# Decoder kernel: expert weights laid out by partition and issued at the logits stage's begin, row stores and a norm on ScalarE, moved loads, waits and bias adds

## Chip, core and metric

The kernel runs on one core of one Trainium2 chip, in one launch. The metric is device time in microseconds (us). The engines are TensorE (PE in the rows; PEld is its weight load), VectorE (DVE), ScalarE (ACT), GpSimd (POOL) and SyncE (SP, which here only issues DMAs).

## Reference

A post-norm decoder of two layers, x of shape (2, 1024, 256), context of shape (2, 154, 192), 16 heads of 16 channels, everything float32. Cut to what matters:

```python
x = layernorm(x + alibi_attention(x))      # half the heads forward, half backward, biased
x = layernorm(x + cross_attention(x, ctx)) # scores clipped to +-10000
x = layernorm(x + moe(x))                  # softmax router, 8 experts, top 2,
                                           # (gelu(x w1) * (x v1)) w2, w1 and v1 256x704, w2 704x256
x = layernorm(x + attention(x))            # full
x = layernorm(x + cross_attention(x, ctx)) # no clip
h = x + mla(rmsnorm(x))                    # causal, keys and values from a latent of 128
x = layernorm(x + h + moe(rmsnorm(h)))     # 8 experts, top 2, silu(x w1) w2, w1 256x512, w2 512x256
```

## The kernel before

The rows of x (2048 tokens of 256 floats) live in SBUF as x_tok, 16 tiles of 128 tokens; two tiles are a pair. The program is a list of 17 stages that run one after another. A counter, stage_done, stands between them (lines 2412 to 2426): each of the five engines ends its part of a stage, drains, adds one, and waits at the next stage until all five have done so. A stage may name one engine that adds its one without draining ("undrained"), and may give SP work that comes behind its drain ("sp_behind"), beside which the other engines go on. The stages are:

- **t0, t1, t4, t5**: token stages (token_stage, line 697). They add the attention's output projection to x, normalise, transpose, and multiply with weights for queries, keys and values, which SP stores to DRAM in the layout that the next stage loads (q_halves, k_parts). A planner (path_lengths, order_by and list_order, lines 93 to 160) sets each engine's order from a table of tasks with costs. t0 also computes keys and values of the context for both cross-attentions (ContextPart), stores the values (line 1284), and loads x (line 1268).
- **at0, at1, mla**: self-attention (self_attention_stage, line 1418): score matmuls of a key block (L1515, L1539, L1542) into one of three PSUM banks, exponential on ScalarE (L1598) into one of four probability buffers, probability-value matmuls (L1557), row maxima on VectorE (L1631), which POOL splits into bfloat16 parts (L1646 to L1653) and SP moves back to be used as an extra row of the next job's scores (L1440). SelfAttention.plan (line 202) writes out the order of these events on TensorE. After the first split POOL adds the projection's bias of the next stage to x_tok (add_bias, L1393: four adds of 128x1024).
- **xa0, xa1**: cross-attention, in sixteen jobs with the same split (L1733 to L1746). xa0 clips the scores: VectorE applies it in L1884. POOL adds the bias after its second split.
- **t2, t6**: token stages whose only product are router logits. After the norm of each pair (task "keep") SP stores that pair's rows to DRAM (x_rows, L841) and then issues a part of the expert weights (between_sp, L2337 to L2355).
- **rt0, rt1**: routing: VectorE picks experts and ranks tokens; POOL's gathers from x_rows (L2088) fetch the tokens of the first experts. SP issues the last four down-projection weights of layer 0 in rt0.
- **ex0, ex1**: experts over 78 tiles of tokens, 39 in each layer; TensorE's first matmul in them is a transpose of fetched rows (L2163).
- **t3, t7**: combine stages (source "comb"): two y rows a token are loaded (y_rows, L834), VectorE adds them with gate weights (L1119), takes mean and variance (L1131, L1134), ScalarE the root (L956), VectorE the reciprocal (L1139) and the norm (L1144). t3 goes on to queries, keys and values; t7 stores the output (L846).

## Time and profile before

| | us |
|---|---|
| median of three runs | 2222.88 (2217.84 to 2225.1) |
| the profiled execution | 2224.16 |
| its span in the profile | 2222.4 |
| TensorE busy in the span | 1953.6 |
| mean granted clock of TensorE | 0.925 of 2.4 GHz |

The stages' begins in the profiled execution, in us of its span: t0 4.4, at0 87.8, t1 364.6, xa0 409.9, t2 558.3, rt0 592.4, ex0 616.8, t3 970.7, at1 1045.4, t4 1462.4, xa1 1506.6, t5 1614.1, mla 1688.1, t6 1955.5, rt1 1991.9, ex1 2013.8, t7 2187.0.

The table by stage gives each engine's busy time in a stage. Where TensorE is busy nearly throughout, only its own idle gaps can be won; where it is not, the timeline and the waits at that place name what it waits for. A group's mean is the price of one instruction. In a timeline row the first number is the start, the second the time that the instructions merged in it took; the bracket has the idle time before them, and what released the engine.

### The profile page before, as it was taken

What the parts mean: (1) busy time and instruction counts of PE and PEld (TensorE: products, weight loads), DVE (VectorE), ACT (ScalarE), POOL (GpSimd) and SP (SyncE); (2) the same over time, 40 slices, a digit from 0 to 9 for tenths busy, and PEclk for the clock granted to TensorE, in tenths of its full rate; (3) what the DMA queues carried; (4) which work ended last, traced back from release to release, by engine and by line L of the source; (5) the groups of instructions that cost most, each with busy time, mean ns of one, the idle gap of its engine ahead of it and who ended that gap; (6) DMA issues with size and microseconds to landing.
All of it is one profiled execution on the core that took longest, in us unless ns stands there. A gap on an engine that the chain in (4) does not pass through costs nothing. (4 is left out here: it accounts for less than half of the span.)

```text
span 2222.4 us, 32846 instructions
## 1 busy us (share of the span) xinstructions
PE 1953.6 (88%) x10990; PEld 1004.1 (45%) x10991; DVE 1294.2 (58%) x2318; ACT 999.2 (45%) x1921; POOL 477.6 (21%) x801
## 2 busy tenths in 40 slices
PE   8699999688669999967999999997887999977992
PEld 4344445333546666643222222253453444464662
DVE  3478784687612222246888888745576887653115
ACT  2156665377211111123466666763542666632331
POOL 2220011522123222212100000023242011033441
PEclk9689999799779999988799999997997999987996
DMA  8522312421730101136211111034225333052223
GB/s 220 137 50 46 62 32 45 101 55 21 278 115 28 33 28 33 28 117 147 34 29 30 30 30 30 2 87 101 46 73 107 59 59 59 2 166 66 63 64 128
DMA packets 111607, 157.90 MB, mean 71 GB/s; under 512 B 31543, under 2 KB 88695, under 8 KB 108535
## 3 DMA queue, kind: packets, MB, share of 16 engines
q1 hardware_dynamic: 103986, 135.75, 26.9%
q0 software_dynamic: 7488, 20.46, 3.0%
q8 instruction: 74, 1.21, 0.3%
q14 instruction: 59, 0.48, 0.1%
HBM read 110.44 MB, written 44.72 MB: 70 GB/s over the span
## 5 line engine op out<-in xcount | busy, mean ns | idle before, releaser
L1598 ACT ACTIVATE arena<-psum 128x512 f32<-128x512 f32 (+1 forms) x1120 | 574.6, 591 | 360.9 <-PE psum L1539 184.2
L1631 DVE TENSOR_REDUCE arena<-psum 128x1 f32<-128x1024 f32 (+3 forms) x352 | 399.9, 1172 | 94.0 <-PE psum L1515 64.9
L1515 PE MATMUL psum<-arena 96*128 96x512 bf16 (+7 forms) x1280 | 366.6, 369 | 31.0 <-DVE arena L1674 12.0
L1539 PE MATMUL psum<-arena 99*128 99x512 bf16 (+7 forms) x1280 | 366.0, 353 | 21.7 <-DMA arena<-arena 13.5
L1617 DVE CUSTOM_DVE_ANT_0 arena<-psum,arena 128x640 bf16<-128x640 f32 (+3 forms) x256 | 250.1, 1022 | 66.6 <-PE psum L1515 65.3
L1557 PE MATMUL psum<-arena 128*32 128x512 f32 (+3 forms) x2560 | 281.5, 538 | 1.1 <-ACT arena L1598 1.1
L2175 PE MATMUL psum<-arena 128*128 x780 | 270.5, 493 | 1.9 <-ACT arena L2229 1.2
L1515 PEld LDWEIGHTS psum<-arena 96*128 96x128 bf16 (+1 forms) x1280 | 100.8, 100 | 272.9 <-issue 82.4
L1539 PEld LDWEIGHTS psum<-arena 99*128 99x128 bf16 (+1 forms) x1280 | 124.6, 99 | 195.9 <-ACT arena L1598 76.4
L2279 DVE COPY arena<-psum 128x640 f32<-128x640 f32 (+1 forms) x78 | 59.3, 760 | 252.6 <-PE psum L2185 252.6
L2194 PE MATMUL psum<-arena 128*128 (+1 forms) x780 | 189.1, 384 | 2.1 <-DVE arena L2282 1.2
L2175 PEld LDWEIGHTS psum<-arena 128*128 128x128 f32 x780 | 143.6, 192 | 82.6 <-issue 25.0
L1646 POOL CAST arena<-arena 32x128 bf16<-32x128 f32 x48 | 13.5, 282 | 757.5 <-DVE arena L1638 757.5
L2194 PEld LDWEIGHTS psum<-arena 128*128 128x128 f32 (+1 forms) x780 | 138.3, 189 | 30.8 <-issue 16.0
L1064 PE MATMUL psum<-arena 128*128 128x512 f32 x240 | 115.2, 621 | 17.3 <-DMA arena<-in_xT 9.8
L2272 DVE TENSOR_TENSOR arena<-arena,psum 128x704 f32<-128x704 f32 x39 | 34.7, 891 | 164.0 <-PE psum L2175 164.0
L2088 POOL DMA_INDIRECT arena<-x_rows,arena x78 | 75.8, 972 | 241.8 <-PE psum L2163 206.6
L1868 DVE TENSOR_REDUCE arena<-psum 128x4 f32<-128x616 f32 x128 | 100.2, 796 | 39.8 <-PE psum L1767 39.2
L1852 ACT ACTIVATE arena<-psum 128x512 f32<-128x512 f32 x160 | 93.7, 604 | 41.8 <-PE psum L1785 40.3
L2124 POOL DMA_INDIRECT y_rows<-arena x78 | 77.0, 987 | 159.0 <-ACT arena L2246 158.7
L1557 PEld LDWEIGHTS psum<-arena 128*32 128x32 f32 x2560 | 59.8, 108 | 111.0 <-issue 65.6
L1542 PE MATMUL psum<-arena 128*128 128x128 bf16 x512 | 98.4, 221 | 0.0
(206 smaller groups left out, 2360.7 us busy)
## 6 DMA issues: line engine op xcount, KB each, us to landing
arena<-k_parts SPq DMA_DIRECT2D x144, 128.0 KB
q_halves<-arena SPq DMA_DIRECT2D x80, 192.0 KB, 3.2
arena<-q_halves SPq DMA_DIRECT2D x40, 384.0 KB, 4.8
arena<-q_halves SPq DMA_DIRECT2D x40, 256.0 KB, 5.2
k_parts<-arena SPq DMA_DIRECT2D x48, 192.0 KB, 3.2
arena<-in_L_ffn_w SPq DMA_DIRECT2D x9, 1024.0 KB, 12.8
arena<-y_rows SPq DMA_DIRECT2D x32, 256.0 KB, 4.1
arena<-in_L_ffn_w SPq DMA_DIRECT2D x8, 704.0 KB, 11.3
```

The costliest lines, as they stand in the source:

```text
L1064: last = nc.tensor.matmul(ps[:, :], m, xt[:, c, :], start=(c == 0), stop=(c == DC - 1))
L1515: last = nc.tensor.matmul(dst[:, base + lo:base + hi], q[0:rows, qh, h, qb % 4 * P:qb % 4 * P + P], k[0:rows, h, key0 + lo:key0 + hi], sta ...
L1539: last = nc.tensor.matmul(b[:, at0:at0 + width], kk[0:rows, h, kb * P:kb * P + P], q[0:rows, qh, h, c0:c1], start=True, stop=diag is None)
L1542: last = nc.tensor.matmul(b[:, at0 + diag - c0:at0 + diag - c0 + P], identb, mask_right if at.modes[g] == "bwd" else mask_left, start=Fals ...
L1557: last = nc.tensor.matmul(bank[o_bank][32 * h:32 * h + 32, c0:c1], v_st[g % 2][:, kb, h, :], probs[k % 4][:, h, c0:c1], start=first, stop=end)
L1598: nc.scalar.activation(probs[k % 4][:, heads[0]:heads[-1] + 1, c0:c1], bank[st_bank[no % 3]][:, 0:len(heads) * width].rearrange("p (h q) - ...
L1617: last = nc.vector.tensor_tensor_reduce(out=unread[:, turn % 2, n_h * width:n_h * width + width], in0=src[:, n_h * pitch:n_h * pitch + wid ...
L1631: nc.vector.tensor_reduce(dst, src, AX.X, ALU.max).then_inc(t("taken"), 1)
L1852: nc.scalar.activation(place(j, tile), src, ACT.Exp, scale=QSCALE).then_inc(t("p"), 1)
L1868: nc.vector.tensor_reduce(dst, src, AX.X, ALU.max).then_inc(t("taken"), 1)
L2175: last = nc.tensor.matmul(bank[2 * w + hf][:, 0:half], xT[:, s, c, :], wu[:, ds(e, 1), c, w, hf * half:hf * half + half].rearrange("p o f ...
L2194: last = nc.tensor.matmul(bank[7][:, 0:D], hT[0:fw[f], s, f, :], w2[f][0:fw[f], ds(e, 1), :].rearrange("p o d -> p (o d)"), start=(f == 0) ...
```

## The change

Ten edits; three places where they move instructions are shown behind the diff.

1. The expert weights are laid out so that each partition reads one run: first-layer w1 and v1 together (8 DMAs of 128x2816 elements in place of 16 of 128x2x704), w2 (rows of 2048 elements). All between_sp work stands behind the drain of SP in t2 and t6.
2. The row stores of t2 and t6 are issued by ScalarE (store_rows, task "keep").
3. In combine stages VectorE computes the reciprocal and minus mean times reciprocal (dve_shift); ScalarE applies scale and shift to the two tiles of a pair (act_norm).
4. Combine stages name POOL as the engine that isn't drained.
5. x is loaded in at0, behind its weights 2, in place of t0.
6. The wait for the context's stores (stored) goes from the end of t0 to the begin of t1; VectorE waits for the value stores before it writes its first output of at0.
7. at0 and mla use five probability buffers; at1 keeps four. The plan holds a score back until fewer than that many products are open, and gives products a later due time for pairs.
8. The bias of both cross-attentions is added after the last split, in 16 adds of 128x256. In self-attention it stays.
9. Lines 112 and 113 of the changed kernel raise the rank of one task; SP's order is not moved by it.
10. TensorE waits for the up weights of layer 0 by the new count of DMAs.

```diff
@@ -243,7 +246,7 @@
             if n_st < len(st):
                 k, n = st[n_st]
                 j = self.steps[k][0]
-                if j in landed:
+                if j in landed and len(pvs) > k - self.ahead:
                     ready.append((max(landed[j], exps[n_st - 3] if n_st > 2 else 0.0), at[k] + n * took[k] / HG, "ST"))
             if n_mx < len(mx):
                 _, j, n = mx[n_mx]
...
@@ -260,7 +263,7 @@
                 j = self.steps[n_pv][0]
                 if len(exps) >= done and (j == 0 or len(copied) >= j):
                     ready.append((max(exps[done - 1], copied[j - 1] if j else 0.0), 
-                                  at[n_pv + self.pair - 1] + 1.6 * took[n_pv + self.pair - 1], "PV"))
+                                  at[n_pv + self.pair - 1] + 1.6 * self.pair * took[n_pv + self.pair - 1], "PV"))
             open_now = [(k, r, w) for r, k, w in ready if r <= now + 0.05]
             if open_now:
                 _, _, what = min(open_now)
...
@@ -752,7 +755,8 @@
                             task("POOL", "spread", p, 1.05, 0.2, ("moments", p))
                         else:
                             task("ACT", "root", p, 0.35, 0.15, ("moments", p))
-                        task("DVE", "norm", p, 0.85 if source == "proj" else 1.1, 0.15, ("spread", p), ("root", p))
+                            task("DVE", "shift", p, 0.45, 0.15, ("root", p), ("norm", p - 4))
+                        task("DVE" if source == "proj" else "ACT", "norm", p, 0.85, 0.15, ("spread", p), ("shift", p))
                     if rms is not None:
                         if norm:
                             task("DVE", "again", p, 1.25, 0.15, ("norm", p), ("rms", p - 4))
@@ -764,7 +768,7 @@
                         task("PE", "trx", p, 0.55, 0.2, (normed, p), ("xts", p - 2))
                         task("ACT", "xts", p, 0.65, 0.15, ("trx", p), ("unit", half_end(p // 2 - 2) - 1))
                     if between_sp:
-                        task("SP", "keep", p, 2.5, 2.0, (normed, p))
+                        task("ACT", "keep", p, 0.6, 2.0, (normed, p))
                     if final:
                         task("SP", "final", p, 0.5, 2.0, ("norm", p))
                 for u, (kind, o, f, part) in enumerate(units):
...
                         load_rows(sp, n)
                         if n == 3 and wn is not None and next_weights:
                             load_weights(sp, wn + 1)
-                    elif kind == "keep":
-                        store_rows(sp, n)
-                        if n + 1 < n_pairs:
-                            between_sp(sp, n)
                     elif kind == "final":
                         store_out(sp, n)
                     elif kind == "store":
@@ -882,10 +882,9 @@
             def sp_stored(sp):
...
                     sp.wait_ge(out_sem(place), stored(nqk))
-                if context:
-                    context.stored(sp)
                 if between_sp:
-                    between_sp(sp, n_pairs - 1)
+                    for p in range(n_pairs):
+                        between_sp(sp, p)
 
             def pool_third(pool, u):
                 n = qk_no[u]
...
@@ -956,6 +955,13 @@
                 nc.scalar.activation(rstd[:, 0, ring(p)], mv[:, 0, ring(p), 1], ACT.Sqrt,
                                      bias=eps_col[:, 0:1]).then_inc(t("root"), 1)
 
+            def act_norm(act, p):
+                act.wait_ge(t("shift"), p + 1)
+                for u in (2 * p, 2 * p + 1):
+                    nc.scalar.activation(x_tok[:, u, :], r_tok[:, u % TPB, :], ACT.Identity,
+                                         bias=rstd[:, 1, u % TPB:u % TPB + 1], scale=rstd[:, 0, u % TPB:u % TPB + 1])\
+                        .then_inc(t("xs"), 1)
+
             def act_xts(act, p):
                 act.wait_ge(t("trx_ps"), p + 1)
                 if p >= 4:
...
@@ -1133,13 +1143,16 @@
                     hold(dve, t(f"st{n}"), 2 * p + i + 1, t("held_dve"))
                     nc.vector.bn_aggr(mv[:, n, 2 * (p % 4) + i, :], bst[:, n, 2 * (p % 4) + i, :]).then_inc(t(done), 1)
 
+            def dve_shift(dve, p):
+                dve.wait_ge(t("root"), p + 1)
+                nc.vector.reciprocal(rstd[:, 0, ring(p)], rstd[:, 0, ring(p)]).then_inc(t("inverse"), 1)
+                dve.wait_ge(t("inverse"), p + 1)
+                nc.vector.scalar_tensor_tensor(out=rstd[:, 1, ring(p)], in0=mv[:, 0, ring(p), 0], scalar=-1.0,
+                                               in1=rstd[:, 0, ring(p)], op0=ALU.mult, op1=ALU.mult)\
+                    .then_inc(t("shift"), 1)
+
             def dve_norm(dve, p):
-                if source == "comb":
-                    dve.wait_ge(t("root"), p + 1)
-                    nc.vector.reciprocal(rstd[:, 0, ring(p)], rstd[:, 0, ring(p)]).then_inc(t("inverse"), 1)
-                    dve.wait_ge(t("inverse"), p + 1)
-                else:
-                    dve.wait_ge(t("pool_n"), 2 * p + 2)
+                dve.wait_ge(t("pool_n"), 2 * p + 2)
                 for u in (2 * p, 2 * p + 1):
                     nc.vector.tensor_scalar(x_tok[:, u, :], r_tok[:, u % TPB, :], mv[:, 0, u % TPB, 0:1],
                                             rstd[:, 0, u % TPB:u % TPB + 1], ALU.subtract, ALU.mult)\
...
@@ -1223,6 +1238,8 @@
                         context.dve_values(dve, n)
 
             progs = {"sp": sp_prog, "dve": dve_prog, "pool": pool_prog, "act": act_prog, "sp_behind": sp_stored}
+            if source == "comb":
+                progs["undrained"] = "pool"
             if units or source == "proj":
                 progs["pe"] = pe_prog
             stages.append((name, progs))
...
@@ -1265,7 +1282,6 @@
             def load(self, sp):
                 load_context_rows(sp)
                 load_weights(sp, self.wn)
-                sp.dma_start(x_tok, a["x"].rearrange("b (t p) d -> p (b t) d", p=P)).then_inc(sem("x_loaded"), 16)
 
             def store(self, sp, n):
                 t, (l, f) = self.t, self.kunits[n]
...
-                sp.wait_ge(t("vstored"), 16 * 2)
+            def values_stored(self, eng):
+                eng.wait_ge(self.t("vstored"), 16 * 2)
+
+            def stored(self, eng):
+                self.values_stored(eng)
                 for s in range(2):
-                    sp.wait_ge(t(f"scr{s}"), 16 * 4 * 2)
+                    eng.wait_ge(self.t(f"scr{s}"), 16 * 4 * 2)
 
             def pe_keys(self, pe, n):
                 t, ct, (l, f) = self.t, self.ct, self.kunits[n]
...
@@ -1385,13 +1403,13 @@
 
         biased = [0]
 
-        def add_bias(pool, n, row):
+        def add_bias(pool, n, row, step=4):
 
             weights_ready(pool, n)
             pool.wait_ge(sem("x_loaded"), 16)
-            for p in range(0, NT, 4):
-                nc.gpsimd.tensor_tensor(x_tok[:, p:p + 4, :], x_tok[:, p:p + 4, :],
-                                        row.unsqueeze(1).to_broadcast([P, 4, D]), ALU.add)\
+            for p in range(0, NT, step):
+                nc.gpsimd.tensor_tensor(x_tok[:, p:p + step, :], x_tok[:, p:p + step, :],
+                                        row.unsqueeze(1).to_broadcast([P, step, D]), ALU.add)\
                     .then_inc(sem("bias_added"), 1)
                 biased[0] += 1
 
...
@@ -1752,8 +1774,8 @@
                         .then_inc(t("pads"), 1)
                 for j in range(len(at.jobs)):
                     pool_split(pool, j)
-                    if j == 1 and bias:
-                        add_bias(pool, *bias)
+                if bias:
+                    add_bias(pool, *bias, 1)
 
 
             def pe_max(pe, j, n):
...
@@ -2336,26 +2358,24 @@
 
         def up_weights0(sp, first, end):
             for e in range(first, end):
-                for w, src in enumerate((g("L0_ffn_w1"), g("L0_ffn_v1"))):
-                    sp.dma_start(wu0[:, e, :, w, :], src[e].rearrange("(c p) f -> p c f", p=P)).then_inc(sem("up0"), 16)
+                sp.dma_start(wu0[:, e].rearrange("p c w f -> p (c w f)"), g("L0_ffn_up")[:, e, :]).then_inc(sem("up0"), 16)
             if end == NX:
                 down_weights0(sp, (4, 5))
 
         def down_weights0(sp, chunks):
             for n in chunks:
                 r = min(P, F0 - n * P)
-                sp.dma_start(w2_0[n][0:r, :, :], g("L0_ffn_w2")[:, n * P:n * P + r, :].rearrange("e p d -> p e d"))\
+                sp.dma_start(w2_0[n][0:r].rearrange("p e d -> p (e d)"), g("L0_ffn_down")[n * P:n * P + r, :])\
                     .then_inc(sem("down0"), 16)
 
         def weights1(sp, e):
-            sp.dma_start(wu1[:, e, :, 0, :], g("L1_ffn_w1")[e].rearrange("(c p) f -> p c f", p=P))\
-                .then_inc(sem("up1"), 16)
+            sp.dma_start(wu1[:, e].rearrange("p c w f -> p (c w f)"), g("L1_ffn_up")[:, e, :]).then_inc(sem("up1"), 16)
             for n in range(4 if e == NX - 1 else 0):
-                sp.dma_start(w2_1[n], g("L1_ffn_w2")[:, n * P:n * P + P, :].rearrange("e p d -> p e d"))\
+                sp.dma_start(w2_1[n].rearrange("p e d -> p (e d)"), g("L1_ffn_down")[n * P:n * P + P, :])\
                     .then_inc(sem("down1"), 16)
 
         def weights0_wait(pe):
-            pe.wait_ge(sem("up0"), 16 * 2 * NX)
+            pe.wait_ge(sem("up0"), 16 * NX)
             pe.wait_ge(sem("down0"), 16 * 6)
 
...
-        self_attention_stage(at0, (2, W["t1"]["brow"]), lambda sp: load_weights(sp, 2))
+                     ("v", w["wv"], w["bv"])], w, following=at0, context=context_part)
+        def rows_and_weights(sp):
+            load_weights(sp, 2)
+            sp.dma_start(x_tok, a["x"].rearrange("b (t p) d -> p (b t) d", p=P)).then_inc(sem("x_loaded"), 16)
+
+        self_attention_stage(at0, (2, W["t1"]["brow"]), rows_and_weights, context_part.values_stored)
         w = W["t1"]
+
+        def first_context(sp):
+            context_part.stored(sp)
+            load_context(sp, 0)
+
         token_stage("t1", 2, "proj", True, None, [("qk", w["wq"], w["bq"], q_halves)], w,
-                    early_sp=lambda sp: load_context(sp, 0), following=xa0)
+                    early_sp=first_context, following=xa0)
         cross_attention_stage(xa0, (3, W["t2"]["brow"]))
         w = W["t2"]
         token_stage("t2", 3, "proj", True, None, [("logits", w["router"], logits)], w,
```

SP, from the last issues in t2 into rt0, before (x_rows is the store of rows, in_L_ffn_w and in_L_ffn_v are expert weights):

```order
L2340 DMA arena<-in_L_ffn_v 128x2x704
L841 DMA x_rows<-arena 128x2x256
L2340 DMA arena<-in_L_ffn_w 128x2x704
L2340 DMA arena<-in_L_ffn_v 128x2x704
L2347 DMA arena<-in_L_ffn_w 128x8x256
L2347 DMA arena<-in_L_ffn_w 64x8x256
L2347 DMA arena<-in_L_ffn_w 128x8x256 x4
L615 DMA arena<-in_L_attn_W_qkv 128x2x256 x3
```

The same place in the changed kernel, from the last moves of xa0 on:

```order
L1736 DMA arena<-arena 1x16x128 x12
L2361 DMA arena<-in_L_ffn_up 128x2816 x8
L2368 DMA arena<-in_L_ffn_down 128x2048
L2368 DMA arena<-in_L_ffn_down 64x2048
L2368 DMA arena<-in_L_ffn_down 128x2048 x4
L618 DMA arena<-in_L_attn_W_qkv 128x2x256 x3
L618 DMA arena<-in_L_attn_b_qkv 128x256
```

No row store stands on SP any more; all up weights and two down weights follow on each other, with the four others behind the next stage's begin.

POOL in xa0, before, at the end of the second split:

```order
L1744 CAST arena<-arena 32x128
L1746 TENSOR_TENSOR arena<-arena 32x128
L1393 TENSOR_TENSOR arena<-arena 128x1024 x4
L1733 TENSOR_SCALAR arena<-arena 32x128
L1739 CAST arena<-arena 32x128
L1741 TENSOR_TENSOR arena<-arena 32x128
```

POOL in xa0, after, from the end of the last split into t2 (ISA rows are semaphore clears between stages):

```order
L1763 TENSOR_TENSOR arena<-arena 32x128
L1766 CAST arena<-arena 32x128
L1768 TENSOR_TENSOR arena<-arena 32x128
L1411 TENSOR_TENSOR arena<-arena 128x256 x16
L2449 ISA x26
L898 TENSOR_SCALAR arena<-arena 128x2
L901 TENSOR_TENSOR arena<-arena 128x2
```

The adds have left the stretch between split two and three and stand behind the last one, in sixteen pieces.

VectorE in t7, before, from its first combining adds:

```order
L1119 SCALAR_TENSOR_TENSOR arena<-arena 128x256 x8
L1131 BN_STATS arena<-arena 128x6 x2
L1134 BN_AGGR arena<-arena 128x2 x2
L1131 BN_STATS arena<-arena 128x6 x2
L1134 BN_AGGR arena<-arena 128x2 x2
L1139 RECIPROCAL arena<-arena 128x2
L1144 TENSOR_SCALAR arena<-arena 128x256 x2
L1139 RECIPROCAL arena<-arena 128x2
L1144 TENSOR_SCALAR arena<-arena 128x256 x2
```

VectorE in t7, after:

```order
L1129 SCALAR_TENSOR_TENSOR arena<-arena 128x256 x16
L1141 BN_STATS arena<-arena 128x6 x2
L1144 BN_AGGR arena<-arena 128x2 x2
L1141 BN_STATS arena<-arena 128x6 x2
L1144 BN_AGGR arena<-arena 128x2 x2
L1148 RECIPROCAL arena<-arena 128x2
L1150 SCALAR_TENSOR_TENSOR arena<-arena 128x2
L1141 BN_STATS arena<-arena 128x6 x2
L1144 BN_AGGR arena<-arena 128x2 x2
L1129 SCALAR_TENSOR_TENSOR arena<-arena 128x256 x4
```

The norms of 128x256 are gone from VectorE, a 128x2 row stands behind each reciprocal, and the first adds are taken four pairs at once.

## Rows read from the trace of the kernel before

**Rows 1.** page, part 1: busy us (share), instructions
```profile
PE 1953.6 (88%) x10990; PEld 1004.1 (45%) x10991; DVE 1294.2 (58%) x2318; ACT 999.2 (45%) x1921; POOL 477.6 (21%) x801
```

**Rows 2.** table by stage (us, busy (x), clock, DMA share, GB/s): t2, rt0
```profile
558.30:592.40 34.10, 32.26 (x192) 29.29 (x192) 18.94 (x60) 13.36 (x24) 7.57 (x16) 0.86 0.70 259
592.40:616.80 24.40, 3.16 (x34) 2.23 (x34) 20.14 (x64) 0.42 (x2) 3.65 (x10) 0.50 1.07 348
```

**Rows 3.** waits, 592.4 to 640 (us in total, times, longest)
```profile
ACT arena L2229 <- PE psum L2163: 32.8, 2, 30.4
```

**Rows 4.** timeline (start, us, engine, line, operation, [idle before <-releaser]), rt0 to ex0
```profile
614.17 0.17 DVE L2045 TENSOR_TENSOR arena<-arena 128x16 f32<-128x16 f32 x1
...
626.88 0.66 PE L2163 MATMUL psum<-arena 128*128 128x128 f32 x2 [14.68 <-DMA arena<-in_L_ffn_w]
```

**Rows 5.** timeline, the same place in layer 1, rt1 to ex1
```profile
2013.52 0.18 DVE L2045 TENSOR_TENSOR arena<-arena 128x16 f32<-128x16 f32 x1
...
2017.12 0.69 PE L2163 MATMUL psum<-arena 128*128 128x128 f32 x2 [5.45 <-DMA arena<-x_rows,arena]
```

**Rows 6.** timeline of SP, t2 and rt0
```profile
568.43 0.38 SPq L841 DMA_DIRECT2D x_rows<-arena  x1
...
583.08 1.64 SPq L841 DMA_DIRECT2D x_rows<-arena  x1
...
595.66 21.00 SPq L2347 DMA_DIRECT2D arena<-in_L_ffn_w  x6
```

**Rows 7.** DMA, 592 to 616.9, in 40 equal slices
```profile
GB/s 414 412 416 402 412 393 378 429 389 414 409 403 389 383 424 417 410 403 398 380 363 356 346 345 334 178 179 204 189 181 220 296 332 327 339 321 337 345 349 341
```

**Rows 8.** timeline, end of t3 and start of at1
```profile
1036.80 2.14 POOL L894 TENSOR_TENSOR arena<-arena 128x512 bf16<-128x512 f32 x2 [1.53 <-ACT arena L984]
...
1037.92 2.55 SPq L827 DMA_DIRECT2D k_parts<-arena  x4
...
1045.48 0.11 DVE L1674 MEMSET arena<- 128x64 f32 x1 [5.38 <-POOLq L2426]
```

**Rows 9.** instruction groups (busy us, mean ns | idle before), stage t7
```profile
L1144 DVE TENSOR_SCALAR arena<-arena 128x256 f32<-128x256 f32 x16 | 5.9, 410 | 0.3
```

**Rows 10.** timelines of POOL, VectorE and TensorE, start of xa0
```profile
424.24 7.85 POOL L1393 TENSOR_TENSOR arena<-arena 128x1024 f32<-128x1024 f32 x4
...
425.63 7.01 DVE L1884 SCALAR_TENSOR_TENSOR arena<-arena 128x512 f32<-128x512 f32 x1
...
433.41 0.69 PE L1767 MATMUL psum<-arena 96*128 96x154 bf16 x4 [6.05 <-DVE arena L1868]
```

**Rows 11.** instruction groups of VectorE, 540.2 to 548.8, end of xa0
```profile
L1884 DVE SCALAR_TENSOR_TENSOR arena<-arena 128x512 f32<-128x512 f32 x5 | 3.5, 691 | 4.2 <-ACT arena L1852 4.2
```

**Rows 12.** timelines of POOL and TensorE, xa1
```profile
1520.80 7.87 POOL L1393 TENSOR_TENSOR arena<-arena 128x1024 f32<-128x1024 f32 x4
...
1528.62 0.28 POOL L1739 CAST arena<-arena 32x128 bf16<-32x128 f32 x1
...
1533.21 0.39 PE L1785 MATMUL psum<-arena 99*128 99x512 bf16 x1 [2.37 <-DMA arena<-arena]
...
1602.52 0.40 POOL L1746 TENSOR_TENSOR arena<-arena 32x128 bf16<-32x128 f32 x1
```

**Rows 13.** waits, stage t0
```profile
ACT arena L975 <- DMA q_halves<-arena: 19.8, 3, 13.2
```

**Rows 14.** table by stretch, as rows 2, end of t0
```profile
60.80:81.30 20.50, 19.68 (x58) 9.81 (x58) 8.56 (x33) 4.15 (x9) 5.49 (x6) 0.50 0.44 112
```

**Rows 15.** timelines of TensorE and POOL, start of at0
```profile
111.38 0.58 PE L1539 MATMUL psum<-arena 105*128 105x512 bf16 x1 [9.04 <-DMA arena<-arena]
...
112.57 7.88 POOL L1393 TENSOR_TENSOR arena<-arena 128x1024 f32<-128x1024 f32 x4 [14.13 <-DMA arena<-in_L_xattn_bq]
...
125.85 0.28 POOL L1646 CAST arena<-arena 32x128 bf16<-32x128 f32 x1 [5.41 <-DVE arena L1638]
```

**Rows 16.** table by stretch, as rows 2, middle of at0
```profile
112.00:345.00 233.00, 226.94 (x1796) 105.00 (x1794) 181.95 (x339) 142.44 (x279) 30.81 (x68) 0.97 0.28 45
```

40 lines of the change are left out of this document (29 added, 11 removed).

## Prediction

> **What bounds the kernel now.** I read the page first, then a table of busy time by stage, and from there only the places where TensorE stands still. TensorE is busy 88% of the span [rows 1] and the change leaves its arithmetic alone, so what can be won is idle time at joints between stages, in stages without matmuls (routing, last combine), and in stretches at 1.2 GHz that a stall brought on. The table of stages names one joint at once: routing 0 lasts 24.4 us, TensorE works 3.16 of them, and the DMA engines are full (share 1.07), as they are through most of the logits stage (0.70 over a stage whose first third has no transfer) [rows 2]. The waits behind it say what TensorE waits for: 14.7 us for expert weights [rows 3]. Everything else is smaller than 10 us and is read at its own place below.
>
> The sum is made against the profiled execution, 2224.16 us (span 2222.4); the median of the three runs, 2222.88, is 1.3 lower, and I take that off at the end.
>
> **Expert weights.** VectorE ends routing 0 at 614.17 + 0.17 = 614.34, and the first expert matmul starts at 626.88, released by the weights [rows 4]. In routing 1 the weights are there in time, and the first matmul starts 2017.12 - 2013.52 = 3.60 us after the start of the same VectorE instruction, released by the fetched rows [rows 5]. With weights in time experts 0 would start at 614.17 + 3.60 = 617.8: **-9.1**. Are they in time? Now the first weight DMA follows the first row store at 568.4, pairs of weights alternate with stores, and the last six are issued until 616.7 [rows 6]. After the change eight DMAs of 1.44 MB and two down-projection ones are issued from the stage's begin at 558.4, the other four from 592.4. Bytes: 11.5 MB up, 5.8 MB down, 2.1 MB of rows, 19.4 MB in all. The rates while the engines are full are 380 to 429 GB/s, then 178 to 220 in a dip and about 340 at the end, where the 1024-byte packets of the down weights run [rows 7]. At 400 the last byte lands at 558.4 + 48.5 = 607, at 340 at 615.5, both before 617.8; it takes under 327 GB/s to lose anything. Long rows per partition should not be slower than short ones. So the full 9.1; what is late next is the row fetch, and nothing closer than 2 us behind it.
>
> **Row stores on ScalarE** (logits stages). Eight issues of a DMA go into ScalarE's stream in t2, eight in t6. No row of before has a DMA issue on ScalarE; the nearest are SP's issues of the same store, 0.38 us with empty queues and 1.64 under backlog [rows 6]. After the change all of t2's stand under backlog. ScalarE is busy 13.36 of 34.1 us in t2, TensorE 32.26 [rows 2]: TensorE sets the stage, and ScalarE's two thirds of idle time cover 8 x 0.38 = 3 us whole, and 8 x 1.64 = 13 us in part, because the stores stand between the activations that TensorE's next transposes wait for, and wait for VectorE's norm themselves. I take **+0.5** for t2, 0 for t6 (nearer to the empty price, as the store has its own queue), bounds -1 and +9 together.
>
> What a page says to that: the Trainium skill, "DMA: Bandwidth & Descriptors", section "Issuing engines are not separate DMA queues", has DMAs of all issuing engines run on the same 16 engines and interleave, so that issuing on another one saves only the sequencer's time. That speaks against any gain in transfer from moving the stores, and by it a store would wait among 13 MB of weights; rows 7's rates make that some tens of us, which the gather at 614 can stand. It leaves the sum as it is.
>
> **The end of combine stage t3.** Its last POOL work ends at 1036.80 + 2.14 = 1038.9, SP's last store is issued by 1037.92 + 2.55 = 1040.5, yet the next stage starts at 1045.48 with VectorE released by POOL's queue at the line of the drain [rows 8]. POOL is now not drained before it reports. SP is last then, with some 0.4 us to the next instruction: 1040.9 against 1045.4, **-4.5**. Bounds -5 and -2 (if SP's or ScalarE's own drain is late too).
>
> **Last combine stage t7.** VectorE sets it. Sixteen normalisations of 0.410 us, 5.9 us busy, leave it [rows 9]; eight tiny shifts come, some 0.2 us each as its other 128x2 ones: 5.9 - 1.6 = 4.3 less work. Of that the last pair gives back 0.3 (a handoff to ScalarE before the last store) and I leave 0.7 for waits on the square root: **-3.3**, bounds -4.5 and +1. In t3, where the same sixteen leave VectorE but TensorE and four other engines share the stage, 0, bounds -2 and +1.
>
> **Late bias in cross-attention.** Before, POOL's four adds run from 424.24 for 7.85 us. VectorE's clip of line 1884, two inputs in SBUF, starts at 425.63 and takes 7.01 us; its usual time is 0.69 [rows 10, 11]. TensorE then stands for 6.05 us [rows 10]. Without the adds there: -6.2. The new place is after the last split, at 540.2, for sixteen adds of a quarter the size: 7.85 us of work plus sixteen starts, some 8.5. In that time five clips stand [rows 11], two more follow, and the chain clip, matmul, exp is what the stage's end (558.3) hangs on. The row shows VectorE shut out across the boundaries of back-to-back adds, so I expect the same again: a clip held to about 548.8, 5.6 us late, of which the 4.2 us of idle ahead of those clips can take back 1 to 2. **+3.7**, net **-2.5**, bounds -8 and +2. Cross-attention 1 has no clips. There the adds (1520.80, 7.87 us) only hold back POOL's next split to 1528.62, and TensorE's wait for the split's result is 2.37 us [rows 12]: -2.5. Its new adds run from 1602.9 to 1611.4 and the stage ends at 1614.1: hidden, with 2.7 us to spare. **-2.5**, bounds -4 and +1.
>
> The Trainium skill, "SBUF — State Buffer", section "Who interferes with whom", says that the second of a VectorE instruction with two SBUF inputs and a POOL one reading SBUF blocks until the first finishes. The row disagrees: one add takes 1.96 us, the clip was held over more than three. By the page a clip after the change would wait one small add, 0.5 us, and the end would cost about +1 in place of +3.7. That is part of rival B.
>
> **x load and context waits.** The 2 MB of x no longer stand ahead of t0's first stores, for which ScalarE waits 19.8 us in three waits [rows 13]; those come out with work beside them, and TensorE's later gap is one of VectorE's: **-1.5**, bounds -3 and 0. At at0's start SP no longer waits for the context's value stores before it loads group 1, some 3.9 us earlier; TensorE's gap of 9.04 before 111.38 waits for data from such a load [rows 15]: -3.9. But x now comes behind the attention's weights, which landed by 112.5 (ahead of 112.57 [rows 15]) and would at 108.6; its 2 MB at 340 GB/s take 6 us and more beside other loads, so about 116, and the adds, now 112.57 to 120.45, go to about 124; the next split is at 125.85 [rows 15] and would be due at 122: about +2. **-2**, bounds -5 and +1.
>
> **Plan of at0 and mla.** Five probability buffers, and probability-value matmuls placed some four places later. In the stretch after the start TensorE is busy 226.94 of 233.0 us [rows 16]; at most 6 us are idle there, and some of it are joints no order mends. I take **-2** for each of the two stages, bounds -5 and +4 each (a worse order has no ceiling but the idle time that it makes). At1's order is the same in both kernels.
>
> **Sum:** -9.1 + 0.5 - 4.5 - 3.3 - 2.5 - 2.5 - 1.5 - 2 - 2 x 2 = **-28.9**. 2224.16 - 28.9 = 2195.3, and less 1.3: **2194**.
>
> **Rivals.**
> B, more than the sum: POOL's small adds let VectorE in (+1 in place of +3.7), and in t0 or at at0's start the shorter stall leaves the clock up. The stretch 60.8 to 81.3 runs at 0.50 (1.2 GHz) and holds 19.68 us of matmuls, which at 2.4 GHz are some 10 [rows 14]. 2194 - 2.7 - 9 = 2182. For it: that stretch follows a 6 us wait. Against: the wait comes from VectorE, not from a store. Chance 0.18.
> C, ScalarE pays the backlog price: 16 issues x (1.64 - 0.38) = 20 us, half of it in front of transposes, +10: 2204. Chance 0.13.
> C', the new plan costs what it was to give, +4 in place of -2 in both stages: 2194 + 12 = 2206. Chance 0.12.
> E, the weights do not come in time, as the long rows gain nothing and rows, weights and ScalarE's queue hinder each other: the 9.1 stay, 2203. Chance 0.04.
> D, **slower**: ScalarE's store can't be issued until the weight backlog has drained. In t2 12.8 MB stand ahead at 0.4 MB/us, 32 us from 558.4; the first store is due near 568, so ScalarE, and TensorE behind it, stand 22 us, and later stores some 5; in t6 8 MB are 20 us, due 10 after the stage's begin, 10 and 4. 2194 + 41 = 2235. It decides once these stalls pass 29 us (no gain left), and is slower by the measure below from 36. Against it: SP's store under full backlog took 1.64, not tens [rows 6]. Chance 0.03.
>
> **Numbers.** Forecast 0.48 (2194), the rest as above, 0.02 for what I don't see. The range holds B's time and C' with its bounds: 2179 to 2212. A difference of 0.3% (6.7 us) is what a measurement of this kernel can tell from none; all cases but D, and the ends of C and C' together, are below 2216: faster 0.93, same 0.04, slower 0.03.
>
> **What would show it.** Routing 0 to experts 0: first matmul of experts within 4 us of routing's last VectorE instruction, released by fetched rows. T3 to at1: no 5 us wait on POOL's queue. Cross-attention 0: no clip of 7 us near 425, and clips near 543 either 0.7 or several us long (decides B's first half). T0: the clock after 60. T2: length 34 or above 40 (C, D). At0 and mla: TensorE's idle time in the middle, 6 us now. Wrong I would be above all if t2 grew by more than 5, or if a stage I hold unchanged (at1, t4, t5) moved.

## The result, and the profile after

| | before | changed |
|---|---|---|
| median, same session, us | 2221.72 (4 runs) | 2196.57 (4 runs, 2184.7 to 2198.73) |
| ratio, 95% interval | | 0.9883 [0.9858, 0.9907] |
| span of the profiled execution | 2222.4 | 2197.0 |

The forecast was 2194 (2179 to 2212), the time 2196.57. The forecast fall was 28.9 us; measured against the kernel before in the same session it was 25.2 us, and 19.8 us when the changed kernel was run again (e5). The stages say less good things of the working. The table has each stage's length from the profiled executions: before has two (its own and that of e11 below), the changed kernel has those of all the kernels below in which the stage's own instructions, in their own place and order, are the changed kernel's. A stage's length is from the moment the five engines may start it to the next such moment, for t7 to the end of the span. The mean of t0 leaves out the 68.9; with it, it is 76.5.

| stage | before | changed, number of executions, mean | difference | forecast |
|---|---|---|---|---|
| t0 | 83.4, 81.0 | 75.7 to 79.1, eight, 77.4; once 68.9 | -4.8 | -1.5 |
| at0 | 276.7, 276.8 | 272.3 to 274.6, eight, 273.6 | -3.1 | -4 |
| xa0 | 148.5, 146.8 | 144.8 to 149.5, eight, 147.0 | -0.7 | -2.5 |
| t2 | 34.0, 33.9 | 35.9 to 37.4, seven, 36.6 | +2.6 | +0.5 |
| rt0 + ex0 | 378.3, 378.5 | 368.2 to 369.5, seven, 369.1 | -9.3 | -9.1 |
| t3 | 74.7, 76.8 | 73.3 to 76.3, seven, 75.1 | -0.7 | -4.5 |
| at1 | 417.0, 415.7 | 414.5 to 416.7, twelve, 415.3 | -1.1 | 0 |
| xa1 | 107.5, 106.6 | 103.0 to 105.8, eleven, 104.6 | -2.4 | -2.5 |
| mla | 267.3, 267.2 | 266.1 to 270.3, eleven, 267.5 | +0.2 | -2 |
| t6 | 36.4, 36.4 | 33.8 to 37.5, eight, 36.8 | +0.4 | 0 |
| t7 | 35.4, 36.0 | 32.8 to 34.1, twelve, 33.4 | -2.3 | -3.3 |

The stages not listed (t1, t4, t5, rt1, ex1) have means within 0.5 us of the kernel before. The differences of the table add up to -21.2 us, against -28.9 in the forecast.

The largest term stands as it was worked out. Of the changed kernel's timeline at the end of routing 0 (columns as in rows 4):

```profile
607.43 0.17 DVE L2067 TENSOR_TENSOR arena<-arena 128x16 f32<-128x16 f32 x1
...
611.54 0.69 PE L2185 MATMUL psum<-arena 128*128 128x128 f32 x2 [6.07 <-DMA arena<-x_rows,arena]
```

The first expert matmul starts 4.11 us behind the start of routing's last VectorE instruction, released by fetched rows; in [rows 4] that was 12.71 us, released by a weight. The table by stage, t2 and rt0, answers to [rows 2]:

```profile
548.80:585.60 36.80, 35.04 (x192) 31.77 (x192) 18.88 (x60) 13.19 (x24) 7.44 (x16) 0.80 0.98 386
585.60:607.70 22.10, 3.15 (x34) 2.22 (x34) 20.07 (x65) 0.42 (x2) 1.78 (x9) 0.50 0.60 238
```

The weights now move in t2 (share 0.98 for 0.70, 386 GB/s), and routing has 0.60 where it had 1.07. T2 itself is longer, at a lower clock (0.80 for 0.86) with TensorE still busy through it: 14.9 us of it are at 1.2 GHz, for 9.4 before.

The end of t3, answering to [rows 8]: no wait for POOL's queue is left, SP is last, and the joint from VectorE's last instruction to its next takes 1.0 us for 5.4.

```profile
1026.71 0.76 DVE L1201 TENSOR_TENSOR arena<-psum,arena 128x256 f32<-128x256 f32 x2 [0.97 <-PE psum L1088]
1028.47 0.11 DVE L1696 MEMSET arena<- 128x64 f32 x1 [1.00 <-SPq L2456]
```

Cross-attention 0, the new place of the bias adds (timelines of POOL, VectorE and TensorE), answering to [rows 10]:

```profile
524.43 9.54 POOL L1411 TENSOR_TENSOR arena<-arena 128x256 f32<-128x256 f32 x16
...
527.48 7.04 DVE L1906 SCALAR_TENSOR_TENSOR arena<-arena 128x512 f32<-128x512 f32 x1 [3.28 <-ACT arena L1874]
...
536.50 1.94 PE L1828 MATMUL psum<-arena 128*32 128x512 f32 x8 [5.90 <-DVE arena L1906]
```

The stall of [rows 10] has moved, nearly to the tenth: a clip of 7.04 us for 7.01, a gap of TensorE of 5.90 for 6.05. Some ten boundaries between adds went by without letting VectorE in, and the clip ended 0.55 us behind the last add, as the clip in [rows 10] did.

Stage t0, waits and TensorE's timeline, answering to [rows 13]; and t7's groups, answering to [rows 9]:

```profile
ACT arena L981 <- DMA q_halves<-arena: 10.1, 1, 10.1
```

```profile
57.66 1.47 PE L1329 MATMUL psum<-arena 128*128 128x256 f32 x4 [1.98 <-DVE arena L1391]
```

```profile
L961 ACT ACTIVATE arena<-arena 128x256 f32<-128x256 f32 x16 | 8.5, 590 | 3.0 <-DVE arena L1150 3.0
...
L1150 DVE SCALAR_TENSOR_TENSOR arena<-arena 128x2 f32<-128x2 f32 x8 | 1.3, 163 | 0.3
```

The start of at0 (timelines of TensorE and POOL), answering to [rows 15]:

```profile
105.14 0.58 PE L1559 MATMUL psum<-arena 105*128 105x512 bf16 x1 [6.88 <-DMA arena<-arena]
...
112.04 7.88 POOL L1411 TENSOR_TENSOR arena<-arena 128x1024 f32<-128x1024 f32 x4 [17.97 <-DMA arena<-in_x]
119.86 0.28 POOL L1666 CAST arena<-arena 32x128 bf16<-32x128 f32 x1
```

### The profile page after: what moved, and what is told of

Read it like the earlier page. It is cut to its first block and busy times, and to the rows that moved or that the text cites. A ratio compares the mean times of both kernels' runs of the same rounds, so it can differ in the third digit from the quotient of the medians.

```text
span 2197.0 us, 32881 instructions
## 1 busy us (share of the span) xinstructions
PE 1950.5 (89%) x10990; PEld 1009.5 (46%) x10991; DVE 1282.9 (58%) x2302; ACT 1015.5 (46%) x1953; POOL 482.0 (22%) x825
## 5 line engine op out<-in xcount | busy, mean ns | idle before, releaser
L1559 PE MATMUL psum<-arena 99*128 99x512 bf16 (+7 forms) x1280 | 365.9, 354 | 19.4 <-DMA arena<-arena 10.5
L2197 PE MATMUL psum<-arena 128*128 x780 | 270.3, 493 | 1.7 <-ACT arena L2251 1.2
L1874 ACT ACTIVATE arena<-psum 128x512 f32<-128x512 f32 x160 | 93.6, 604 | 38.7 <-PE psum L1807 37.4
```

The costliest lines, as they stand in the source:

```text
L1559: last = nc.tensor.matmul(b[:, at0:at0 + width], kk[0:rows, h, kb * P:kb * P + P], q[0:rows, qh, h, c0:c1], start=True, stop=diag is None)
L1874: nc.scalar.activation(place(j, tile), src, ACT.Exp, scale=QSCALE).then_inc(t("p"), 1)
L2197: last = nc.tensor.matmul(bank[2 * w + hf][:, 0:half], xT[:, s, c, :], wu[:, ds(e, 1), c, w, hf * half:hf * half + half].rearrange("p o f ...
```

## The experiments

Each kernel is the changed kernel with the edit shown, unless it says otherwise. Ratios are to the kernel before in the same session.

**e1: POOL drained again in combine stages.**

```diff
-            if source == "comb":
-                progs["undrained"] = "pool"
```

> The changed kernel with POOL drained at the end of the combine stages again. In the changed kernel t3 lasts 73.3 us and at1 414.6, against 74.7 and 417.0 before. Theory (the drain is worth its wait and the clock that the wait costs): t3 grows by 4.5 us to about 77.8, VectorE again waits about 5.4 us on POOL's queue at the start of at1, and at1's start at 1.2 GHz ends some 2 to 3 us later after its begin, so at1 grows by about 2.4; time +7 (2203). Rival (at1's 2.4 us has another cause, its first loads or the state in which SP comes out of t3): t3 +4.5, at1 unchanged, time +4.5. Second rival (the drain is hidden, as other engines end later in the re-planned t3): t3 +1 to +2.

Median 2206.64, ratio 0.9944 [0.9921, 0.9967]. T3 78.94 us, at1 414.97. The wait is back (timeline of VectorE at at1's start):

```profile
1028.29 0.11 DVE L1694 MEMSET arena<- 128x64 f32 x1 [5.53 <-POOLq L2454]
```

Against the seven t3 of the changed kernel (mean 75.1) the drain costs 3.8 us, and 2.7 against the longest of them. At1 is as without it: the 2.4 us that at1 seemed to gain are not the drain's. In the stages this is the first rival. The median rose by 10 us, more than either gave; that rest is in no stage of the profile (span 2200.3 for 2197.0 and 2199.3), whose execution was the fastest of this kernel's seven, and stays open.

**e2: norm of t3 on VectorE.** The plan's tasks and dve_norm as before where the stage is not the final one.

```diff
-                            task("DVE", "shift", p, 0.45, 0.15, ("root", p), ("norm", p - 4))
-                        task("DVE" if source == "proj" else "ACT", "norm", p, 0.85, 0.15, ("spread", p), ("shift", p))
+                            if final:
+                                task("DVE", "shift", p, 0.45, 0.15, ("root", p), ("norm", p - 4))
+                        if source == "comb" and not (final):
+                            task("DVE", "norm", p, 1.1, 0.15, ("root", p))
+                        else:
+                            task("DVE" if source == "proj" else "ACT", "norm", p, 0.85, 0.15, ("spread", p), ("shift", p))
```

> The changed kernel with the norm of t3 on VectorE again (reciprocal and subtract-multiply, planned as before); t7 keeps it on ScalarE. Up to its last store t3 took 70.2 us before (1040.9 - 970.7) and 73.3 in the changed kernel. Theory (putting the norm on ScalarE costs t3 its new 3 us, as ScalarE's queue then delays the evictions that TensorE waits for): t3 falls to 70 to 71, time -3 (2193.5). Rival (the 3 us come from the start of t3, that is from the order of the first combining adds or the loads, whoever does the norm): t3 stays at 73 +-0.7. t7 32.6 +-0.3 in both.

Median 2194.04, ratio 0.9889 [0.9852, 0.9927]. T3 69.76 us; e9, e10 and e12 below, which share the edit, have 69.5, 69.7 and 68.5 (e12 has another edit in t3). So the norm on ScalarE costs t3 5 to 6 us of its 75.1, more than expected, and t7, which keeps it, stays at 33.4. Part of that is the clock: five of the changed kernel's seven t3 (75.4 to 76.3) have a second stretch of 3.4 us at 1.2 GHz near 66 us, which no t3 of these four has. Against the two without it (73.3 and 73.7) the norm costs 3.5 to 4.2 us, e12 left out. The median does not show the gain: 0.9889 lies between the changed kernel's 0.9883 and 0.9907, and only the span (2190.4 for 2197.0 and 2199.3) does. The first 20 us of t3, of this kernel and of the changed one (columns as in rows 2), show that TensorE gets less done from the start:

```profile
950.10:970.10 20.00, 8.35 (x18) 4.28 (x19) 12.81 (x38) 3.44 (x8) 0.00 (x0) 0.57 0.79 243
```

```profile
955.10:975.10 20.00, 6.11 (x13) 3.28 (x14) 12.90 (x42) 5.26 (x13) 0.00 (x0) 0.53 0.78 243
```

The groups of ScalarE over t3 have the cause as far as it shows: sixteen activations of 128x256 that take VectorE 410 ns each [rows 9] take ScalarE 591, in a queue that also holds TensorE's evictions.

```profile
L961 ACT ACTIVATE arena<-arena 128x256 f32<-128x256 f32 x16 | 8.7, 591 | 1.3 <-DVE arena L1150 1.3
```

TensorE's first matmul of t3 comes 11.5 us after the begin in the changed kernel and 10.9 here, and behind it TensorE idles 9.4 us and 6.6: together 3.4 of the 3.5 us between the two profiles. Its largest gap in t3 (3.36 us, here 1.57) stands behind VectorE, VectorE behind an eviction of ScalarE, and that behind a store of q_halves (6.79 us, here 4.31).

**e3: a wait before each late bias add.**

```diff
             for p in range(0, NT, step):
+                if step < 4 and p:
+                    pool.wait_ge(sem("bias_added"), biased[0])
```

> The changed kernel with one wait ahead of each of the sixteen bias adds in the cross-attentions: POOL waits for the add before it. In the changed kernel the adds ran 9.54 us back to back and a clip of VectorE took 7.04 us beside them. Theory (VectorE is shut out as long as POOL's adds follow each other without a pause; a wait in between lets it in): the clips take at most 1.4 us each, TensorE's gap of 5.9 us shrinks to 1 or 2, xa0 147.6 -> 143 to 144, time -4 (2192.5). Rival (it is not the queueing of adds but POOL's reading that slows VectorE, in proportion to the time shared): a clip still takes over 3 us or the sum of the clips' extra time stays near 6, xa0 unchanged. POOL's adds take longer, some 11 to 12 us in all; in xa1, with 2.7 us to spare, they may end after the others: xa1 +0 to +1.

Median 2196.94, ratio 0.9875 [0.9829, 0.9921]. Cross-attention 0 137.68 us. Timelines of POOL and VectorE at the place of the stall:

```profile
523.65 14.68 POOL L1413 TENSOR_TENSOR arena<-arena 128x256 f32<-128x256 f32 x16
...
525.88 1.08 DVE L1908 SCALAR_TENSOR_TENSOR arena<-arena 128x512 f32<-128x512 f32 x1 [3.29 <-ACT arena L1876]
...
532.79 1.02 DVE L1908 SCALAR_TENSOR_TENSOR arena<-arena 128x512 f32<-128x512 f32 x1 [1.46 <-ACT arena L1876]
```

A clip takes 0.68 to 1.13 us beside POOL's adds, against 0.69 alone and 7.04 beside adds that follow on each other; the nine clips beside them lose 2.9 us together, where the rival had 6. Being shut out is a matter of adds queued without a pause. The price is on POOL, 14.68 us for 9.54. The stage's 9.9 us are more than the stall, as its stretches at 1.2 GHz fell from 29.5 to 18.8 us in this execution; in e9, e10 and e12, with the same wait in xa0, it took 141.7, 141.4 and 143.6, against a mean of 147.0, so 3.4 to 5.6 us are the edit's. The median did not follow: t3, at1 and xa1 were 1.6 to 3.1 us longer in the profile than in the changed kernel's. For t3 and at1, not edited, that is within the scatter of the table. Xa1, which has the waits too, took 106.3 us, 0.5 over the longest without them, and ended with POOL's last add (1588.56 and 1588.63): there the waits cost something.

**e4: less weight backlog in t2.**

```diff
-                    for p in range(n_pairs):
+                    for p in range(n_pairs if name == "t6" else 5):
                         between_sp(sp, p)
...
-        routing_stage("rt0", True, "t2", "ex0", lambda sp: down_weights0(sp, (0, 1, 2, 3)))
+        routing_stage("rt0", True, "t2", "ex0", lambda sp: (up_weights0(sp, 5, NX), down_weights0(sp, (0, 1, 2, 3))))
```

> The changed kernel with the up weights of five experts issued at t2's begin and those of the last three, with the down weights, only in routing 0. t2 took 34.05 us before and 36.8 in the changed kernel, where the last two row stores held ScalarE's queue 5.7 us and the clock fell 25.3 us after t2's begin (28.1 before). 4.3 MB move by some 25 us: the last byte at about 605, first expert matmul then still released by fetched rows (611.5). Theory (backlog price): the row stores take under 1 us each, t2 falls to 34 to 35, time -2. Rival (ScalarE's place in the plan, not the backlog, costs it): t2 stays 36.5 or more. Rival (what the shorter t2 gains comes back as waiting for weights in experts 0): rt0 and ex0 together grow by the same 2.

Median 2202.01, ratio 0.9925 [0.9895, 0.9956]. ScalarE's issue of the last row store took 0.37 us, where it takes 3.70 in the changed kernel (rows under e8), and t2 stayed at 36.85 all the same: the clock had fallen 25.4 us after its begin, and TensorE's wait for ScalarE's last evictions was 0.69 us in both, as before. And the deferred weights came late (timelines of ScalarE and TensorE):

```profile
575.20 0.37 ACTq L845 DMA_DIRECT2D x_rows<-arena  x1
```

```profile
614.30 0.66 PE L2185 MATMUL psum<-arena 128*128 128x128 f32 x2 [10.43 <-DMA arena<-in_L_ffn_down]
```

That is 8.2 us after routing's end (606.07), and ex0 is 4.0 us longer. The estimate of a last byte at 605 was too early: the up weights of five experts and the rows are through by 577, and the DMA engines move nothing more until 584.

**e5: the changed kernel again,** nothing edited.

> The changed kernel once more, nothing edited, to learn how far a stage's length moves between executions of the same program. Expected by both theories: at0, t1, xa0, rt0, t7 within 1 us of 273.4, 45.0, 147.5, 22.0, 32.6; t3 either near 73.3 or near 76.2 (both lengths were seen for this code), going with the length of its stretch at 1.2 GHz (20.5 or 23.9 us); xa1 103 to 105, again with its stretch at 1.2 GHz. Theory (the kernel's total moves by several us only by which stretches the clock is low): span 2190 to 2200, and the difference to 2197.0 is found in t3, xa1, t5 and t6. Rival: the lengths are fixed, and t3's 73.3 against 76.2 in two kernels edited elsewhere is an effect of these edits; then t3 is 73.3 again.

Median 2199.65, ratio 0.9907 [0.9879, 0.9934]. Span 2199.3. T3 75.36, xa1 103.03, at0 273.74, t7 33.03, rt0 22.00; xa0 149.51, 2.0 above the first, with 38.1 us at 1.2 GHz for 29.5. So t3's 73.3 in the first profile was its short end, and a single profile tells nothing of a stage under 2 to 3 us unless the clock's stretches are the same.

**e6: x loaded in t0 again.**

```diff
                 load_weights(sp, self.wn)
+                sp.dma_start(x_tok, a["x"].rearrange("b (t p) d -> p (b t) d", p=P)).then_inc(sem("x_loaded"), 16)
...
             load_weights(sp, 2)
-            sp.dma_start(x_tok, a["x"].rearrange("b (t p) d -> p (b t) d", p=P)).then_inc(sem("x_loaded"), 16)
```

> The changed kernel with the load of x back in t0; the moved waits stay as they are. In the changed kernel t0 takes 78.4 us (83.4 before), its large gap 1.98 us in place of 6.12. Theory (x ahead of the first stores made ScalarE wait, and VectorE's late answer after it opened the gap): t0 back to 82 to 83.5, its gap 5 to 6 us. At0: bias adds begin some 5 us earlier than 29.2 us after at0's begin, at0 -1 to 0. Time +3 to +4 (2200). Rival (the gap closed because SP no longer waits at t0's end and the plan's order around it, not by x): t0 stays near 78.4.

Median 2197.66, ratio 0.9899 [0.9878, 0.992]. T0 81.04, at0 270.79. Waits of t0 and TensorE's and POOL's timelines:

```profile
ACT arena L981 <- DMA q_halves<-arena: 17.7, 3, 11.7
```

```profile
59.07 2.37 PE L1330 MATMUL psum<-arena 128*128 128x256 f32 x4 [3.58 <-DVE arena L1392]
```

```profile
107.01 7.88 POOL L1412 TENSOR_TENSOR arena<-arena 128x1024 f32<-128x1024 f32 x4 [10.50 <-DMA arena<-in_L_xattn_bq]
```

The rival is out (t0 is 1.9 above the longest with x in at0), and the theory holds in direction, not in size: x in t0 costs t0 3.7 us and saves at0 2.8, where 4 to 5 and 0 to 1 were expected, so that the move is worth under 1 us. The gap was 3.58, not 5 to 6. But the kernel before had it at 2.90 in its second execution (e11), so that the 6.12 of the forecast's rows was its long end. ScalarE's wait and TensorE's gap move together, one for one: of the thirteen executions of all kernels here with such a wait (all but e12's), twelve have a gap of the wait less 8.2 us. It is 11.07 and 2.90 in e11, 11.7 and 3.58 here, 10.1 and 1.98 in the changed kernel; the one left out has 13.2 and 6.12.

**e7: the old plan of at0 and mla.**

```diff
-        self.ahead = 4 if modes[0] == "full" else 5
+        self.ahead = 4
...
-                if j in landed and len(pvs) > k - self.ahead:
+                if j in landed:
...
-                                  at[n_pv + self.pair - 1] + 1.6 * self.pair * took[n_pv + self.pair - 1], "PV"))
+                                  at[n_pv + self.pair - 1] + 1.6 * took[n_pv + self.pair - 1], "PV"))
```

> The changed kernel with the plan of before for at0 and mla: four probability buffers, no hold on scores, products due as before. At0 took 276.7 and mla 267.3 before, 273.4 and 266.1 in the changed kernel, which had at0's earlier begin of loads besides. Theory (the order gives about 1 to 2 us in each): at0 274.5 to 275.5, mla 267 to 268, time +2 to +3. Rival (the order gives nothing, at0's 3.3 us are those of its earlier loads, mla's 1.2 are scatter): at0 273 to 274, mla 266 to 267, time within 1.

Median 2199.98, ratio 0.9916 [0.9893, 0.9939]; span 2193.5. At0 275.50, 0.9 above the longest of eight and 1.9 above their mean: a gain of 1 to 2 us from the plan, by this one execution. Mla 269.86 lies inside what the new plan gave (266.1 to 270.3), and the old plan took 267.3 and 267.2 in the two executions of before: no gain can be shown there. This run's t0, unedited, took 68.9 us. It is the one execution of that code without a stretch at 1.2 GHz, and the one with the shortest wait of ScalarE for the store, 8.35 us (table by stretch; TensorE's timeline):

```profile
4.50:73.30 68.80, 61.29 (x224) 33.45 (x224) 33.60 (x78) 24.22 (x41) 20.26 (x20) 1.00 0.72 184
```

```profile
54.61 1.32 PE L1329 MATMUL psum<-arena 128*128 128x256 f32 x4 [0.19 <-DVE arena L1391]
```

**e8: weights laid out as before, issued early.** The 16 up DMAs, down DMAs and the counts of before in up_weights0, down_weights0, weights1 and weights0_wait, and no re-layout.

```diff
-                sp.dma_start(wu0[:, e].rearrange("p c w f -> p (c w f)"), g("L0_ffn_up")[:, e, :]).then_inc(sem("up0"), 16)
+                for w, src in enumerate((g("L0_ffn_w1"), g("L0_ffn_v1"))):
+                    sp.dma_start(wu0[:, e, :, w, :], src[e].rearrange("(c p) f -> p c f", p=P)).then_inc(sem("up0"), 16)
```

> The changed kernel with the expert weights laid out as before (16 DMAs of 2816-byte packets for layer 0's up weights, 1024-byte packets for the down weights), issued from t2's begin as in the changed kernel. In the changed kernel the DMA engines are done some 50 us after t2's begin, the first expert matmul starts at 611.5, 3.9 us after routing 0's last VectorE instruction, released by fetched rows. Theory (the early issue gives the gain, the layout is not needed for it): at 340 to 410 GB/s the last byte lands by 606, the first matmul starts within 4.2 us of routing's end, rt0 and ex0 as in the changed kernel within 1 us; time within 1.5. Rival (the short packets, at 180 to 340 GB/s in routing 0, make the weights late): the matmul waits for a down weight and starts 3 to 10 us later, time +3 to +10.

Median 2199.3, ratio 0.9921 [0.9893, 0.9948]. The first expert matmul starts 4.06 us after routing's end (602.72), released by fetched rows, and rt0 and ex0 take 369.1 us together: the early issue is all of the gain. T2 took 33.93 us, as before: the stores on ScalarE cost it nothing here. TensorE's first expert matmul; the issue of a store by ScalarE, and the stores' landing over the first 17 us of t2 (DMA issues, us to landing), here and then in the changed kernel:

```profile
573.88 0.37 ACTq L845 DMA_DIRECT2D x_rows<-arena  x1
```

```profile
606.78 0.69 PE L2185 MATMUL psum<-arena 128*128 128x128 f32 x2 [6.25 <-DMA arena<-x_rows,arena]
```

```profile
x_rows<-arena ACTq DMA_DIRECT2D x4, 256.0 KB, 8.4
```

```profile
576.79 3.70 ACTq L845 DMA_DIRECT2D x_rows<-arena  x1
580.59 1.15 ACT L970 ACTIVATE arena<-psum 128x512 f32<-128x512 f32 x2 [6.48 <-PE psum L1053]
```

```profile
x_rows<-arena ACTq DMA_DIRECT2D x4, 256.0 KB, 19.3
```

With packets of 2816 bytes on SP's queue a row store lands in 8.4 us, with the long rows of the new layout in 19.3. Seven of the eight issues take about 0.4 us with either layout; with the long rows the last one, of the stage's last pair, is held 3.7 to 4.9 us (not in e4, where fewer such rows stand ahead).

**e9: three parts altered.** The edits of e2 and e8, and e3's wait in cross-attention 0 alone (`if pause and p:`, pause given as at.clip).

> The changed kernel with three of its parts altered at once: expert weights laid out as before (issued from t2's begin), norm of t3 on VectorE, and in cross-attention 0 alone a wait of POOL for the add before each bias add. In single kernels these gave t2 33.9 for 36.8, t3 69.8 for 73.3 to 76.2, xa0 137.7 for 147.5. Theory (the parts add up, and nothing that depends on the clock takes them back): t2 34, t3 70 to 72, xa0 138 to 141, xa1 103 to 106, t7 33, span 2178 to 2186, time 11 to 19 under the changed kernel. Rival (TensorE's clock, low in other stretches when more work is done per time, gives part of it back, as the total of the kernel with the waits alone, 2196.9, seems to say): the three stages shrink as said, but other stages grow, time 2190 or more.

Median 2188.0, ratio 0.9856 [0.9829, 0.9883], lower than the changed kernel's 0.9883 and 0.9907, though its interval meets theirs. T3 69.5, xa0 141.7, but t2 36.9 in place of 34: the clock fell 25.0 us after its begin (table by stretch), though no store held ScalarE long.

```profile
540.50:577.40 36.90, 35.11 (x192) 32.07 (x192) 18.87 (x60) 13.32 (x24) 7.44 (x16) 0.79 1.01 383
```

So t2 has two prices, which don't add. In every execution the clock is at 1.2 GHz at its end; what differs is from when, and whether there is a stretch of 3.4 us early in the stage as well. Short packets, 9.1 to 9.5 us at 1.2 GHz in all, the last stretch from 28 us after the begin: 33.9 (e8), 34.0 (e10), and the kernel before 34.0 and 33.9. Long rows, 9.1 us, from 27 us: 35.9 and 36.0 (e7, e2), where TensorE's gap behind ScalarE is 3.49 and 3.61 us for 0.69, behind a store held 4.84 and 4.92. About 15 us at 1.2 GHz, from 25 us: 36.8 to 36.9 with either layout (e4, e5, e6 and the changed kernel with long rows, e9 and e12 with short), TensorE's gap 0.69 even where the store is held. E1 and e3, with long rows and 14 and 12 us, have 37.4 and 36.5. The rows of e7:

```profile
564.08 4.84 ACTq L845 DMA_DIRECT2D x_rows<-arena  x1
```

```profile
570.15 2.09 PE L1093 MATMUL psum<-arena 128*128 128x8 f32 x9 [3.49 <-ACT arena L970]
```

Whether the change brings on the earlier fall is not shown: it came in kernels with either layout.

**e10: e9 with x loaded in t0 behind at0's first loads.**

```diff
                         load_first(sp, following)
+                        if context:
+                            sp.dma_start(x_tok, a["x"].rearrange("b (t p) d -> p (b t) d", p=P)).then_inc(sem("x_loaded"), 16)
```

> The kernel of the run before this one, with x loaded in t0 behind the loads of at0's first group (issued near 35 to 40 us), in place of in at0. With x in at0, its stage took 272.3 to 274.5 us, with x at t0's begin 270.8; t0 then took 81.0 in place of 75.7 to 79.1. Theory (x costs t0 only if it stands ahead of the first stores, and costs at0 only by POOL's late bias adds): t0 76 to 79, at0 270 to 271.5, time -2.5 against the run before this one. Rival (any 2 MB in t0 are in the way of the later stores): t0 79 or more, time within 1 of the run before.

Median 2195.72, ratio 0.9895 [0.9867, 0.9923]. T0 84.6, at0 273.6. The rival's t0 (79 or more) came true, by more than it said; the time rose by 7.7 us, more than either gave. And at0 did not shrink, though POOL's bias adds began 22.5 us after its begin, against 21.5 in e6: so e6's 270.8 is not the early adds alone, and what it is stays open. Timelines of SP and ScalarE in t0:

```profile
41.95 10.52 SPq L835 DMA_DIRECT2D q_halves<-arena  x4
```

```profile
57.27 0.69 ACT L987 ACTIVATE arena<-psum,arena 128x512 bf16<-128x512 f32 x1 [15.62 <-DMA q_halves<-arena]
```

SP's four store issues took 10.5 us behind x, the first alone 8.37, ScalarE waited 15.6 us for them, and TensorE's gap was 7.46. That led to the last experiment: the store is late because of what stands ahead of it on SP.

**e11: the kernel before again,** nothing edited.

> The kernel before once more, nothing edited, to learn the scatter of its stages, as the run of the changed kernel alone was repeated. Differences under one microsecond in a stage are then scatter. Theory (the changed kernel's gains in at1 (-2.4) and xa1 (-4.2) are partly which stretches ran at 1.2 GHz): at1 between 414.5 and 417.5, xa1 105.5 to 107.5, t6 either near 36.4 or 37.4, mla 267 to 269, t3 74 to 77. Rival (they are fixed effects of the change): at1 417.0 and xa1 107.5 again within 0.5. In both: t0 83 to 84, rt0 24.5, ex0 353.9, t7 35.2.

Median 2218.22, ratio to itself 0.9995 [0.9976, 1.0014]. At1 415.7, xa1 106.6, t3 76.8, t6 36.4, t0 81.0 (2.4 under its first, with TensorE's gap at 2.90 us for 6.12). So at1's -2.4 was half scatter, and xa1's -4.2 is -2.4 by the means.

**e12: e9 with at0's and at1's first loads later on SP.**

```diff
-                    task("SP", "ahead", 0, 5.0, 3.0, *[("store", v) for v in qk_no if v < half_end(1)])
+                    task("SP", "ahead", 0, 5.0, 3.0, *[("store", v) for v in qk_no
+                           if v < half_end(1) or nqk == 16 and qk_no[v] < nqk // 2 + 4])
```

> The kernel of e9_three with one edit: in t0 and t3 the loads of the next attention's first group, for which SP first waits until the first half's stores have landed, are placed four store units later in SP's order. In t0 ScalarE waits 10.1 us (13.2 before) until 51.8 for a store whose issue stands on SP behind that wait and these loads (issued from 41.5), and TensorE's gap at 55.7 follows from it; in t3 the same wait is 4.0 us. Theory (the gap of t0 is the late store, passed on by ScalarE and VectorE): ScalarE's wait shrinks to under 7 us, no gap of 1 us near 55, TensorE's clock falls later or not at all, t0 76.3 -> 69 to 74, time -2 to -7 against 2188.0. Rival (the store's landing, not its issue, sets the wait, as queues are full then): wait and t0 as in e9_three (75.7 to 79). T3 69.5 +-1 in both; at0 and at1 +0 to +1, if their first group lands late.

Median 2183.24, ratio 0.9836 [0.982, 0.9852], the lowest of all and clear of the changed kernel's, though not of e9's. The stores are now issued from 39.17 on (41.5 in the changed kernel, the second four from 42.6), ScalarE waits under 1.8 us for anything between 45.4 and 58.8, TensorE has no gap of 0.9 us until t0's end, and t0 takes 70.1 us (timeline of SP; table by stretch):

```profile
39.17 2.96 SPq L836 DMA_DIRECT2D q_halves<-arena  x4
42.60 3.07 SPq L836 DMA_DIRECT2D k_parts<-arena  x4
```

```profile
4.50:74.50 70.00, 62.19 (x224) 33.98 (x224) 34.26 (x78) 24.86 (x41) 20.20 (x20) 0.99 0.72 181
```

Of the 6.3 us under e9's t0, 1.8 are its gap and the rest is the clock, 0.99 for 0.91 (1.3 us at 1.2 GHz for 13.7). The twelve executions with a gap of 1.09 us or more there have 13.7 to 23.9 us at 1.2 GHz, from 53 to 57 us into the stage on; the two without one, e7 and e12, have 0 and 1.3. At0 and at1 take 273.4 and 416.0: their loads are early enough.

## Why the prediction was right, and where it was not

**Expert weights** (-9.1): right in size, cause and in what is late next (-9.3; fetched rows). The rates used for the bound were the right ones; the layout part of it was worth nothing for this, as e8 shows (4.06 us, 369.1). It had a price that was not foreseen, on the row stores (next point).

**Row stores on ScalarE** (+0.5): mis-sized, +2.6 in t2 and +0.4 in t6, within the bound of 9. The empty price, taken on the ground that the store has its own queue, was right for all issues in t6 and seven of eight in t2, some 0.37 us each. The step that failed is to give every store that price: beside rows of 11 KB the last store of t2 was held 3.7 to 4.9 us, which cost TensorE up to 2.9 us (e2, e7), with 2816-byte packets it was not held, and t2 took what it took before (e8, 33.9). The clock, which the term does not have, is the other half: in e9 and e12 t2 was 36.9 and 36.8 with no store held, and in the changed kernel's own profile TensorE waited no longer for ScalarE than before (0.69 us), while it was busy 35.04 us for 32.26 at the lower clock: all of its +2.8 is the clock. T6's +0.4 goes with the clock too: 36.3 with 12.6 us at 1.2 GHz (e3, e10), as before, and 33.8 with 6.6 (e4).

**End of t3** (-4.5): the joint was worked out rightly (5.4 us to 1.0), and e1 gives the drain 3.8 us. But t3 as a whole gained 0.7. The step that failed is that of the **norm in t3**, put at 0 with a bound of +1: it cost 5 to 6 us (e2), 3.5 to 4.2 without t3's second stretch at 1.2 GHz. Among the executions without that stretch the two terms account for t3: 74.7 before, 69.5 to 69.8 without the drain and with the norm on VectorE, 73.3 and 73.7 in the changed kernel. The forecast counted VectorE's relief and did not price ScalarE's 0.59 us each in front of evictions; 16 x 0.59 = 9.4 us were put on the queue that TensorE waits for, while VectorE had slack (49.7 of 69.8 us busy in e2).

**T7** (-3.3): -2.3, the same mechanism, in a stage where VectorE is the bound. ScalarE's norm is 0.59 for 0.41 us, and the last two pairs are normalised one after the other (2.07 us), where 0.3 was allowed.

**Cross-attention 0** (-2.5): -0.7. The stall moved as forecast and was longer, the clip 6.35 us late for 5.6: the adds took 9.54 us, not 8.5. The reading that an unbroken row of adds shuts VectorE out, against the section "Who interferes with whom" of the Trainium skill's "SBUF — State Buffer", which has the second instruction wait for the first to finish, is borne out: 7.04 us beside sixteen small adds, at most 1.13 beside the same adds with a pause (e3). **Cross-attention 1** (-2.5): -2.4, the new adds hidden. Among executions with 21 to 22 us at 1.2 GHz it is -1.6, so some of it is the clock.

**T0** (-1.5): the step that failed is "TensorE's later gap is one of VectorE's", and not of a store. VectorE stood behind ScalarE, ScalarE behind a store of q_halves, and the store behind SP's earlier work. The wait is the longest of the three that the forecast quotes from [rows 13], 13.2 us. Each us that the store came earlier was a us off the gap: 11.1 to 10.1 against 2.90 to 1.98, and the like in ten more executions. E12 shows it from the other side. Rival B's clock, argued for t0, was real in one execution of nine (68.9 us), and in the one profile of e12; its other half, small adds that let VectorE in, was not.

**At0's start** (-2) and **plan** (-2): together -3.1 for -4. TensorE's first long gap was 9.04 and 9.61 us before and 5.8 to 8.9 in ten executions with x in at0 (mean 6.9), so that the earlier loads gave some 2.4 us there for the 3.9 worked out. Late x cost 2.8 us by e6 for the 2 worked out, but e10 leaves open by what; the plan gave 1 to 2, by one execution (e7). **Mla** (-2): nothing that can be shown. The forecast read only at0's busy share [rows 16] and gave mla the same; a bound on the idle time didn't say that there was something to win.

That the total was near is in part luck. Misses cancelled in part: t0 and at1 gave 4.4 us more than said, t2, t3, at0, xa0, mla, t6 and t7 some 12 less, so that the stages say -21 for -28.9. The rest is the scatter of a session's median: -25.2 where the forecast was tested, -19.8 in the repeat (ratios 0.9883 and 0.9907 for the same program). Of the rivals, C's price of 1.26 us more for each issue was seen nowhere; D's cause, a store held by the backlog, in one issue of sixteen, and for under 5 us; E's only where weights were deferred (e4).

## What to carry to other kernels

Before moving work to an idle engine, ask what else stands in its queue there: the same edit gave 2.3 us in a stage that VectorE bounds and cost 5 to 6 where ScalarE feeds TensorE. Follow a wait through all the engines that pass it on, down to the DMA queue that issues the transfer; t0's gap, named as VectorE's, was gone once four store units stood ahead of the next loads on SP. When a bulk transfer is packed into long rows, look at the small transfers that share the engines. And before a stage's difference of 2 or 3 us is put down to an edit, compare executions with as much time at 1.2 GHz.

## What the runs showed of the hardware that I had not expected

A VectorE instruction with two inputs in SBUF took 7.04 us, across some ten boundaries of POOL adds of 0.6 us each, and 0.68 to 1.13 us when POOL waited on a semaphore between them. The same 256 KB store on ScalarE's queue landed in 8.4 us beside 2816-byte packets and in 19.3 beside 11264-byte rows, at a like total rate (about 400 GB/s); one issue in eight then held ScalarE 3.7 to 4.9 us in place of 0.37. On SP a store issued right behind the 2 MB of x was held 8.37 us (e10), where the same issue took 0.58 without x in front (e9). And a stage whose own instructions were not edited moved by 3 us or more; in t0 the length goes with the stretch at 1.2 GHz, 13.7 to 17.7 us and once none: t0 75.7 to 79.1 and once 68.9, cross-attention 0 144.8 to 149.5, mla 266.1 to 270.3.
